# Cross-attention and expert feed-forward on one core: half of the second expert layer in three reduced passes, and a load of output weights cut in two

## The reference

```
assign = argmax(x @ centroids.T)
h      = relu(xn @ w1[e].T + b1[e])        # 256 -> 1024
y      = x + h @ w2[e].T + b2[e]           # 1024 -> 256
out    = a * y + (1 - a) * x,   a = sigmoid(x @ centroids[e])
```

## Time and profile before

| | |
|---|---|
| median of 3 runs | 1070.32 us (1070.15 to 1070.99) |
| the profiled execution's own time | 1066.71 us |
| its span in the trace | 1064.9 us |
| mean granted TensorE clock | 0.999 of full speed |
| TensorE, VectorE, ScalarE, GpSimd busy | 99%, 75%, 63%, 46% |
| HBM traffic over the span | 105 GB/s |

### The profile page before, as it was taken

How to read it: one execution, slowest core, us unless ns; L and a number is a source line. 1 busy time by engine, 2 the same in 40 slices (tenths; PEclk the granted TensorE clock), 3 DMA queues, 4 the chain that set the end, 5 groups by cost and what they waited for, 6 DMA issues and landing times.

```text
span 1064.9 us, 24086 instructions
## 1 busy us (share of the span) xinstructions
PE 1051.3 (99%) x8454; PEld 941.1 (88%) x8454; DVE 796.3 (75%) x1907; ACT 670.9 (63%) x1820; POOL 494.8 (46%) x647
## 2 busy tenths in 40 slices
PE   8989999999999999999999999999999999999998
PEld 6879898988888888989898888888898999999997
DVE  7867888888888988888888888898886554544441
ACT  6765757585676766575757567676555646656551
POOL 2744464646454555546464645455445342222222
PEclk9999999999999999999999999999999999999999
DMA  6576667585757676766658575766367657767670
GB/s 209 120 194 148 165 166 189 139 218 139 207 144 185 150 194 163 188 161 174 181 146 213 145 206 139 190 149 157 90 170 226 236 196 249 240 223 232 227 260 28
DMA packets 159660, 190.51 MB, mean 179 GB/s; under 512 B 17453, under 2 KB 149037, under 8 KB 154672
## 3 DMA queue, kind: packets, MB, share of 16 engines
q1 hardware_dynamic: 155088, 179.09, 61.6%
q0 software_dynamic: 3360, 8.53, 2.2%
q10 hardware_dynamic: 1088, 1.31, 0.4%
HBM read 65.72 MB, written 46.07 MB: 105 GB/s over the span
## 4 chain that ended last, share of the span: by engine, by line
PE 94%; POOL 2%; DVE 2%; DMA 1%; issue 1%; ACT 0%; SPq 0%; POOLq 0%; DVEq 0%
PE psum L698 17%; PE psum L731 16%; PE psum L873 12%; PE psum L768 11%; PE psum L858 10%; PE psum L747 9%; PE psum L783 9%; PE psum L717 8%; PE psum L786 1%; POOL prob L1701 1%; POOL w_o_lo L1758 0%; DVE neg_max L1307 0%; DMA prob_t<-r_ring 0%; POOL r_ring L1701 0%; DMA c_in<-in_ctx_in 0%
## 5 line engine op out<-in xcount | busy, mean ns | idle before, releaser
L1701 POOL TENSOR_TENSOR prob<-prob,inv_sum 128x512 f32<-128x512 f32 x172 | 179.4, 1057 | 195.9 <-DVE inv_sum L1313 195.5
L1307 DVE TENSOR_REDUCE neg_max<-psum 128x2 f32<-128x512 f32 x256 | 162.2, 673 | 36.8 <-PE psum L747 36.8
L1052 ACT ACTIVATE prob<-psum,neg_max 128x256 f32<-128x256 f32 x344 | 160.4, 479 | 32.3 <-DVE neg_max L1307 31.7
L873 PE MATMUL psum<-w,v_n 128*128 128x256 f32 x608 | 134.2, 379 | 0.0
L1319 DVE STREAM_TRANSPOSE prob<-prob 128x512 f32<-128x512 f32 x172 | 118.5, 699 | 12.1 <-POOL prob L1701 11.7
L873 PEld LDWEIGHTS psum<-w,v_n 128*128 128x128 f32 x608 | 114.2, 190 | 14.8
L1701 POOL TENSOR_TENSOR w_ring<-w_ring,inv_sum 128x512 f32<-128x512 f32 x76 | 78.2, 1042 | 79.8 <-DVE inv_sum L1313 79.8
L1059 ACT ACTIVATE head_out_hi<-psum 128x512 fp32r<-128x512 f32 x52 | 31.0, 597 | 118.8 <-PE psum L768 103.0
L1775 POOL DMA_INDIRECT out<-x_in,r_ring x38 | 39.6, 1043 | 130.3 <-DVE x_in L1551 129.6
L1038 ACT ACTIVATE v_n<-psum 128x512 f32<-128x512 f32 x128 | 77.9, 609 | 27.4 <-PE psum L731 22.6
L1027 ACT ACTIVATE k_hi<-psum 128x512 fp32r<-128x512 f32 x128 | 77.1, 603 | 19.1 <-PE psum L698 17.8
(11 more groups left out here) (189 smaller groups left out, 2712.1 us busy)
## 6 DMA issues: line engine op xcount, KB each, us to landing
sorted_rows<-filler SPq DMA_DIRECT2D x54, 660.0 KB, 5.0
prob_t<-prob SPq DMA_DIRECT2D x172, 128.0 KB, 2.8
w_ring<-prob SPq DMA_DIRECT2D x172, 128.0 KB
w<-in_experts SPq DMA_DIRECT2D x19, 1024.0 KB
w_ring<-in_experts SPq DMA_DIRECT2D x18, 1024.0 KB, 5.9
prob_t<-w_ring SPq DMA_DIRECT2D x76, 128.0 KB, 2.8
w_ring<-w_ring SPq DMA_DIRECT2D x76, 128.0 KB
w_ring<-normed SPq DMA_DIRECT2D x56, 128.0 KB, 3.0
```

The source lines that it names most:

```text
L873: last = pe.matmul(bank[:, 0:d_model], hid[:, s % 2, f, i * P:(i + 1) * P], w2[:, f * d_model:(f + 1) * d_model], start=(f == 0), stop=(f ...
L1052: act.activation(prob_at(u, bb)[:, :, parity, i], scores_i, ACT.Exp, bias=neg_max[:, at, i:i + 1], accum_out=prob_sum[:, at, i:i + 1]).the ...
L1307: dve.tensor_reduce(neg_max[:, (4 * u + n) % 8, :], psum[:, n, :].rearrange("p (i j) -> p i j", i=2), AXIS_X, ALU.max, negate=True).then_i ...
L1701: pool.tensor_tensor(probs, probs, inverse, ALU.mult).then_inc(s_soft, 1)
```

## The change

In the attention part, `load_w_out_t` takes its half as an argument: half 0 is loaded in step 1 once the projection weights are split, half 1 in step 2, after the move of step 1's second half and ahead of step 2's first, once two pieces of `w_out` are split. The pieces are split in the opposite order, upper half of the raw place first. In step 4 `high_centroids` and `low_centroids` go ahead of the last exponentials and of their reciprocal.

In the feed-forward, from block 4 on (`FIRST_SPLIT`), `layer_2_split` takes four of the eight chunks of the hidden layer in three fp32r passes and the other four in plain fp32. For that, `relu_parts` writes chunks 0 to 3 to a raw place and 4 to 7 to a plain one, VectorE's `split_hidden` makes their high and low halves, ScalarE's `high_weights_2` and GpSimd's `low_weights_2` those of half of the second weights. `finish` adds in place of `upd`. VectorE transposes the rows of block `s+3` ahead of `finish(s)`. On SP, `load_vectors` no longer waits for output rows, `load_rows` does; the order becomes `move_rows(s)`, `load_vectors(s+1)`, `load_rows(s+1)`, `load_weights_1(s+2)`, `load_weights_2(s)`, `load_b2(s)`.

```diff
@@ SP
-                def load_w_out_t():
-                    sp.wait_ge(s_wlo, len(pieces))
-                    sp.wait_ge(s_wo_split, 2 * W_OUT_PIECES)
-                    for h in range(2):
-                        sp.dma_start(w_o_t[h], w_out_t[:, :, h * half:(h + 1) * half]).then_inc(s_wo_t, 16)
+                def load_w_out_t(h):
+                    if h == 0:
+                        sp.wait_ge(s_wlo, len(pieces))
+                    else:
+                        sp.wait_ge(s_wo_split, W_OUT_PIECES)
+                    sp.dma_start(w_o_t[h], w_out_t[:, :, h * half:(h + 1) * half]).then_inc(s_wo_t, 16)
...
                     if u > 0:
                         move_probabilities(u - 1, 1)
+                    if u == 2:
+                        load_w_out_t(1)
...
                     if u < n_steps:
                         move_probabilities(u, 0)
-                    if u == 2:
-                        load_w_out_t()
+                    if u == 1:
+                        load_w_out_t(0)
...
+                load_weights_2(n_early - 1)
+                load_b2(n_early - 1)
                 scattered(n_batches)
                 run = block_steps(sp, count_empty(sp))
-                for s in range(n_early, n_slots + 1):
-                    run(s, (load_vectors,), (load_rows,), (load_weights_1,))
-                    run(s - 1, (load_weights_2,), (load_b2,))
+                run(n_early, (load_vectors,), (load_rows,), (load_weights_1,))
+                run(n_early + 1, (load_weights_1,))
+                for s in range(n_early, n_slots):
                     run(s, (move_rows,))
+                    run(s + 1, (load_vectors,), (load_rows,))
+                    run(s + 2, (load_weights_1,))
+                    run(s, (load_weights_2,), (load_b2,))
@@ TensorE
+                def layer_2_split(s):
+                    pe.wait_ge(f_w2h, s - FIRST_SPLIT + 1)
+                    pe.wait_ge(f_w2l, s - FIRST_SPLIT + 1)
+                    pe.wait_ge(f_hl, FS // 2 * (s - FIRST_SPLIT + 1))
+                    pe.wait_ge(f_ha, FC // 2 * s)
+                    def in_parts(bank, i, first):
+                        for n, (hw, hx) in enumerate(PASSES):
+                            for f in range(FS):
+                                last = pe.matmul(bank, hid_hl[hx][:, s % 2, f, i * P:(i + 1) * P], w2_hl[s % 2][hw][:, f, :], ...)
+                    def plain(bank, i, first):
+                        for f in range(FS, FC):
+                            last = pe.matmul(bank, hid_plain[:, s % 2, f - FS, i * P:(i + 1) * P], w2_ring[s % NW2][...], ...)
+                    bank = begin(("fy", s, 0))[:, 0:d_model]
+                    in_parts(bank, 0, True)
+                    plain(bank, 0, False).then_inc(f_y, 1)
+                    bank = begin(("fy", s, 1))[:, 0:d_model]
+                    plain(bank, 1, True)
+                    in_parts(bank, 1, False).then_inc(f_y, 1)
@@ ScalarE
+                def high_weights_2(s):
+                    act.wait_ge(f_w2[s % NW2], 16 * (s // NW2 + 1))
+                    if s < FIRST_SPLIT + 2:
+                        wait_made(act, ("wout", n_batches - 1))
+                    else:
+                        wait_made(act, ("fy", s - 2, 1))
+                    act.activation(w2_hl[s % 2][0], ..., ACT.Copy).then_inc(f_w2h, 1)
...
+                    if u == 4:
+                        high_centroids()
                     exponentials(u, 3)
...
                     run(s + 2, (normalise_rows,), (high_weights_1,))
-                    run(s + 1, (relu,))
+                    run(s + 1, (relu_parts,))
                     run(s + 2, (row_gain_bias,))
+                    run(s + 1, (high_weights_2,))
@@ VectorE
+                def split_hidden(s):
+                    for i in range(FS // 2):
+                        dve.wait_ge(f_ha, FC // 2 * (s - 1) + i + 1)
...
+                        then_next(dve.tensor_copy(hi, hid_raw[:, i, :]))
+                        dve.tensor_tensor(lo, hid_raw[:, i, :], hi, ALU.subtract).then_inc(f_hl, 1)
...
-                    run(s + 2, (transpose_rows,), (low_weights_1,), (split_xn,))
+                    run(s + 2, (low_weights_1,))
+                    run(s + 1, (split_hidden,))
+                    run(s + 2, (split_xn,))
+                    run(s + 3, (transpose_rows,))
                     run(s, (finish,))
@@ GpSimd
+                def low_weights_2(s):
+                    pool.wait_ge(f_w2h, s - FIRST_SPLIT + 1)
+                    raw = w2_ring[s % NW2][:, 0:FS * d_model].rearrange("p (f d) -> p f d", f=FS)
+                    pool.tensor_tensor(w2_hl[s % 2][1], raw, w2_hl[s % 2][0], ALU.subtract).then_inc(f_w2l, 1)
...
                         run(s + 2, (add_base,))
+                        run(s + 1, (low_weights_2,))
                         write_rows(s)
```

More of the change, by code:

```diff
@@ L35 @@
 NW, NW2, NR = 2, 3, 4
+FIRST_SPLIT = 4
 W_OUT_PIECES = 4
@@ L179, in build @@
             k_s = [sbuf(a, f"k_{h}", [P, 2, 2, BANK], F32R) for h in ("hi", "lo")]
+            FS = FC // 2
+            with ExitStack() as late:
+                hid_hi = sbuf(late, "hid_hi", [P, 2, FS, BLOCK], F32R)
+                sbuf(late, "hid_between", [P, 3 * FS * BLOCK])
+                hid_lo = sbuf(late, "hid_lo", [P, 2, FS, BLOCK], F32R)
             v_n = sbuf(a, "v_n", [P, 2, 2, 2, BANK])
@@ L876, in layer_2 @@
                         last.then_inc(f_y, 1)
+                def layer_2_split(s):
[6 more added lines that the diff above has]
+                            for f in range(FS):
+                                last = pe.matmul(bank, hid_hl[hx][:, s % 2, f, i * P:(i + 1) * P], w2_hl[s % 2][hw][:, f, :],
+                                                 start=(first and n == 0 and f == 0), stop=(not first and n == 2 and f == FS - 1))
+                        return last
+                    def plain(bank, i, first):
+                        for f in range(FS, FC):
+                            last = pe.matmul(bank, hid_plain[:, s % 2, f - FS, i * P:(i + 1) * P],
+                                             w2_ring[s % NW2][:, f * d_model:(f + 1) * d_model],
+                                             start=(first and f == FS), stop=(not first and f == FC - 1))
+                        return last
+                    bank = begin(("fy", s, 0))[:, 0:d_model]
[4 more added lines that the diff above has]
+                    in_parts(bank, 1, False).then_inc(f_y, 1)
                 pe.wait_ge(s_blank, 1)
@@ L961, in _ @@
                         row_transposes(s + 2)
-                    layer_2(s)
+                    if s < FIRST_SPLIT:
+                        layer_2(s)
+                    else:
+                        layer_2_split(s)
                 run = block_steps(pe, count_empty(pe))
@@ L965, in _ @@
                     run(s + 1, (layer_1,))
-                    run(s, (layer_2,))
+                    run(s, (layer_2_split,))
             @block.scalar
@@ L1154, in relu, with relu_parts @@
                                 ins.then_inc(f_ha, 1)
+                def relu_parts(s):
+                    b1 = vec_ring[:, s % NR, 2 * KC:]
+                    if s == FIRST_SPLIT:
+                        wait_low(act, n_pairs - 1, 1)
+                    for i in range(FC // 2):
+                        act.wait_ge(f_h, FC // 2 * (s - 1) + i + 1)
+                        if i < FS // 2 and s > FIRST_SPLIT:
+                            act.wait_ge(f_hl, FS // 2 * (s - 1 - FIRST_SPLIT) + i + 1)
+                        elif i == FS // 2:
+                            wait_made(act, ("fy", s - 2, 1))
+                        for f in (2 * i, 2 * i + 1):
+                            at = slice((f % 2) * BLOCK, (f % 2 + 1) * BLOCK)
+                            dst = hid_raw[:, i, at] if f < FS else hid_plain[:, s % 2, f - FS, :]
+                            ins = act.activation(dst, psum[:, i, at], ACT.Relu, bias=b1[:, f:f + 1])
+                        ins.then_inc(f_ha, 1)
+                def high_weights_2(s):
+                    act.wait_ge(f_w2[s % NW2], 16 * (s // NW2 + 1))
+                    if s < FIRST_SPLIT + 2:
+                        wait_made(act, ("wout", n_batches - 1))
+                    else:
+                        wait_made(act, ("fy", s - 2, 1))
+                    act.activation(w2_hl[s % 2][0], w2_ring[s % NW2][:, 0:FS * d_model].rearrange("p (f d) -> p f d", f=FS),
+                                   ACT.Copy).then_inc(f_w2h, 1)
                 act.dma_start(c_in[:, 0:2, :], ctx_in[0:2].rearrange("b p d -> p b d")).then_inc(s_in[0], 16)
@@ L1246, in _ @@
                     high_weights_1(s + 2)
-                    relu(s + 1)
+                    relu_parts(s + 1)
                     row_gain_bias(s + 2)
+                    high_weights_2(s + 1)
                 run = block_steps(act, count_empty(act))
@@ L1749, in split_w_out @@
                 def split_w_out(i):
[L1751 removed]
```

(3 more changed lines are left out.)

41 lines of the change are left out of this document (27 added, 14 removed).

## The result

| | before | after |
|---|---|---|
| median, 20 runs each | 1069.5 us (1067.54 to 1071.09) | 1074.01 us (1068.98 to 1076.76) |
| the profiled execution, its span | 1066.71, 1064.9 us | 1074.85, 1073.1 us |

The ratio is 1.0039, with a 95% interval of 1.0028 to 1.0050. The changed kernel is 0.4% slower; 1% faster was forecast.

What follows compares the result with a forecast made beforehand. TensorE was taken as the bound, busy 99% of the span. Savings of 8.7 and 2.55 us, 11.3 together, took the median carried as 1070.3 to 1059.0, plus 0.2 for tails: 1059.2 us, range 1056.8 to 1064.5.

Steps and rivals of the forecast that it cites:

- What the other engines take on: Late blocks: the split's new work on ScalarE, VectorE and GpSimd fits their room and order, priced at 0.
- the ring: Late blocks: finish, output rows land, SP fetches rows, ScalarE normalises, VectorE transposes before the next finish; 11.6 us against 12.08.
- rival A: Late blocks: output loop takes over, slower than before; 13.44 us a turn eats the gain; chance 0.05, milder form 0.09.
- R: Late blocks: time of one turn of the loop through output rows, summed to 11.6 us.
- The split: Second layer, blocks 4 to 18: half the products in three fp32r passes save TensorE 0.58 us a block, 8.7 us.
- B: Late blocks: the split costs TensorE 0.19 us more a block for type changes or waits; 1062.2 us, chance 0.10.
- D: Second layer's parts: fp32r matmuls take 0.107 us each, so the split saves 13.5 us; 1054.3 us, chance 0.02.
- the 0.2 us for tails: End of the blocks: added for tails such as the change of matmul kind between the last two blocks.
- The join: Attention part: earlier output-weight loads remove a 2.15 us TensorE wait, earlier centroid columns 0.4 us; together 2.55 us.
- rival C: Attention part: the stall only moves, some 0.5 of 2.55 us remains; 1061.2 us, chance 0.07.
- SP's queue: Late blocks: rows ahead of weights and first weights one block earlier, worth 0 since TensorE waits for no load.
- The formula 12 x (R - P) - 5: Late blocks: loss over 12 turns if R exceeds P, TensorE's own turn (12.08 us), less about 5 us of slack.

Runs made afterwards that it cites:

- e5: Changed kernel with VectorE's finish(s) ahead of transpose_rows(s+3) and low_weights_1(s+2) behind split_hidden(s+1): 1056.51 us against 1069.36 before, ratio 0.9881.
- e4: Kernel before with only the attention part of the change (output weights loaded in halves, centroid columns earlier): 1064.14 us against 1069.53, ratio 0.9952.
- e6: Changed kernel with finish(s) put back ahead of transpose_rows(s+3) and SP's queue in the order of the kernel before: 1058.38 us against 1069.36, ratio 0.9893.
- e9: Like e5, but with SP's queue in the order of the kernel before: 1057.67 us against 1069.85, ratio 0.9882.
- e1: Changed kernel with VectorE's finish(s) put back ahead of transpose_rows(s+3), all else kept: 1060.01 us against 1069.53, ratio 0.9910.

## Why the prediction was wrong

**The step that failed** is in "What the other engines take on": "I price all of this at 0", said with the reminder that the dearest "goes into the ring of rival A", and in that rival the ring's first term, "914.86 to SP at 919.61 is 4.75". The ring was counted from the right places, in the right order, and given 0.5 us to spare. Its other terms held: 2.79 for 2.62, 1.60, some 0.7 and 1.8 for 1.9. The first was 6.40 us, since it had been read in a turn whose second write met nothing on VectorE, while the change puts `low_weights_1` right behind `finish`, where the write falls and is held for 2.1 us. Then R is 13.3 in a turn and 13.8 in the mean, where rival A had put 13.44 for a gain eaten whole. A is what happened; it had a chance of 0.05.

**Why it got so little.** I took the contention between GpSimd and VectorE for a matter of tenths, by the longest of 18 subtractions, and asked "the ring would have to be 1.9 us longer than its rows". The prediction never looked at the longest of the writes: in before's list that is 2.76 us against a median of 0.99, the row shown above. The page cited there, the Trainium skill's "GPSIMD Engine Reference", section 8, says only that there is contention. The Trainium skill's "SBUF — State Buffer", section "SBUF: two separate sides", says how: the two engines' common pair of ports goes to one instruction whole, as a lock, and while VectorE runs an fp32 copy from SBUF to SBUF, a DMA issued from GpSimd's queue can't get its descriptors written.
**The split** was right. The parts' matmuls cost 0.120 us, no change of kind shows in the 12.09 us of a turn (rivals B and D are out; D's 1054.3 left out the 0.2 us for tails that the other sums have), and in e5 it is worth 7.6 us of 8.7, with the other new orders in it.

**The join** was right in its mechanism and size in the profiled execution, 2.9 us in e4 for 2.55, and rival C is out. Mis-sized was its share of the median, 5.4 us: "I carry it over", said of the 3.6 us between median and profiled execution, took as a fixed offset what was mostly the stall that the join removes. That is why e5's 1056.51 is below the 1059.2 forecast for a change without a ring: the join gives 2.9 us more in the median than was summed, the split 1.1 less, and the median before is 1069.5 where the sum began at 1070.3.

**SP's queue** at 0 can't be told from what e6 and e9 show, 1.6 us one way and 1.2 the other. The formula 12 x (R - P) - 5 with the right R would have given about 1071 for the profiled execution, against 1074.85: the right sign, and 3.9 us short.

## What to carry to other kernels

When a change shortens the bounding engine's turn, add up every loop that passes through other engines, with its longest instances as well as its medians, and look at which long instructions the new order puts beside each term. An indirect write from GpSimd belongs beside short VectorE instructions; the order of VectorE's steps in a turn was worth 17.5 us here (e5 against the changed kernel). A median that lies above the profiled execution is itself a cost to be found: profile the same kernel again before carrying the gap over.

## What the runs showed of the hardware

GpSimd's indirect write ended 0.85 to 0.89 us after the end of the VectorE instruction beside it, with a two-input subtraction of 128x2048, one of 128x512, a two-input maximum and a one-input copy, and took 0.97 to 1.03 alone. The write at 960.03 above, 1.05 us, began under a one-input cast of 128x512 (959.82, 0.42 us) and ended 0.84 us after it. Over the traces of all runs, 88 indirect writes of the block stretch began while `low_weights_1` ran; 86 were held and ended 0.83 to 0.90 us after it. Of the other two, one began 0.07 us before its end, and one 0.03 us behind its start (886.98 above), and there the subtraction took 2.35 us for its usual 2.29. A transposition of 128x512 held none of the 43 writes that began under it (in the kernel before, 0.98 us at 903.00 under one from 902.64 to 903.35).

The hold works the other way too. In e1 an instruction of VectorE with three operands took 2.11 us in place of 0.49 beside GpSimd's subtraction, and ended 0.29 us after it:

```profile
959.35 2.65 POOL L1878 TENSOR_TENSOR w_o_lo<-w,w_o_hi 128x1024 fp32r<-128x1024 f32 x1
```

```profile
960.18 2.11 DVE L1647 SCALAR_TENSOR_TENSOR x_in<-x_in,r_ring,base 128x256 f32<-128x256 f32 x1
```

In e1 and in e5 nearly every turn has such an instruction, and e5 is the fastest run all the same. GpSimd's subtraction of 128x1024 took 2.40 us in the changed kernel, 2.6 having been counted. A stall of 2.2 us left TensorE's granted clock at 1.00, and one of 2.9 or 3.5 us was followed by 0.75 and 0.64 over the next 6 us.
